# Storing one-hot columns of an adjacency matrix in five transfers, and loading them back on another queue

## The chip, the cores and the metric

The kernel runs on one core of a Trainium2 chip. The metric is the device time of one execution in microseconds (us). TensorE does the matrix products, VectorE and ScalarE move and transform tiles, GpSimd does small powers and indirect gathers, SyncE issues most of the transfers between the core's own memory and DRAM. SyncE and ScalarE each have a queue of their own for transfers; each engine runs its own instructions in program order.

## What is computed

A graph of 3125 nodes and 50000 edges, 256 features per node, four layers with a skip connection:

```python
edge_index = jnp.stack([src, dst])
h = jnp.maximum(_layernorm(x, axis=-1), 0.0)
x = x + _L0_gnn_ref(h, edge_index, ...)   # means over edges, there and back, two times
h = jnp.maximum(_layernorm(x, axis=-1), 0.0)
x = x + _L1_gnn_ref(h, ..., src, dst, edge_type_16)   # sum of messages, then a GRU cell
h = jnp.maximum(_layernorm(x, axis=-1), 0.0)
x = x + _L2_gnn_ref(h, edge_index, ...)   # GCN with self loops, layer norm, relu
h = jnp.maximum(_layernorm(x, axis=-1), 0.0)
x = x + _L3_gnn_ref(h, edge_index, ...)   # attention over four heads
```

## The kernel before

Nodes are cut into 25 tiles of 125. The dense adjacency matrix `k.adj` (125 partitions, 25 row tiles of 3200 bytes, 8-bit floats, 128 bytes for each column tile) stays in the core's memory. It is built from the edge list in `build`; all later stages are in `main`. Every engine has one function there (`sync`, `gpsimd`, `tensor`, `scalar`, `vector`), and what it issues is written out by hand in program order, with semaphores between engines. The stages in `tensor` are, in this order:

- **back1** (13 pairs of tiles, `back1(p)`): products with the transposed adjacency. The transposed tiles are made on the fly. `flip` on TensorE transposes a tile `i` in seven pieces, `flip_out` on ScalarE (even pieces) and VectorE (odd pieces) moves them into slot `i % 4` of `k.big`, and `keep(i)` on SyncE stores the slot to DRAM (`adjTp`) for later use. While `back1(p)` runs, the tiles of pair p+1 are flipped. Before `flip_out` writes the slot again, for tile i+4, it waits for that store (`kept[i % 4]`) and for the products of the pair that read it. On SyncE `store_g(i - 6)` follows each `keep(i)`: two stores of a finished row tile.
- **mean2**, then **back2** (transposed tiles loaded back on ScalarE's queue by `load_at`).
- **gru** with the GRU cell: `cell` on TensorE, then on VectorE `biases(i)`, `cell(i-1)`, `reset(i)`, `low_s(i-1)`, and on ScalarE `gates(i)`, `split_s(i-1)`, `squash(i)`. SyncE stores each finished tile to `x2p` and loads the input of the tile after the next (`load_x1`), and until the tile is number 18, a `load_hold` six tiles ahead.
- **gcn**, with `dense_c`, `turn_h` (a transpose of the normalized tile) and `dense_z` between the products; on VectorE `norm_c(i)`, which needs the tile that `load_x2(i)` brings back from `x2p`. The products that stand before `turn_h` of tile 1 are few, since three pairs begin ahead of time with the tiles that are ready.

Five of the adjacency's column tiles (19 to 23) play a special part. High node numbers get most of the edges, so in mean2 and gru the tiles of high number are summed from gathered rows and one-hot matrices (`far_mean2`, `far_gru`) rather than from the dense columns. The one-hot matrices (`hots`, written by `far_hots` on VectorE) need room, and they take these columns' place, `hot_columns`. So the columns are stored to the DRAM tensor `columns` before mean2 and loaded back before the gcn stage uses them. They are 125 partitions x 25 row tiles x 640 bytes, 2 MB in pieces of 640 bytes. VectorE waits for the semaphore `G["columns"]` before its first `far_hots` and again in the gcn loop at tile 3, where after `one_hots()` it adds the self loops of those columns. The last reader of the one-hot matrices is the last far group of the gru stage (`FAR_TURNS[-1]`, turn 11 of 13); its end is the count `F["used"]` that `copy_out` on ScalarE waits for in that turn.

In the version before, both transfers are issued by SyncE: the store as one transfer (L749) ahead of the loads of `attn_r` and `attn_l` (L751) and `keep(2)`, the load (L793) between `load_x2(0)` and `load_x2(1)` (L734).

Of the kernel before, what the change touches and what calls it, by code (L numbers as in the profile page):

```python
# [26 lines left out]
TILES = NODES // P  # L27
# [134 lines left out]
def visiting():  # L162


    out = []
    for stage, order, tiles in ((0, MEAN_ORDER, range(MEAN_FAR, TILES)), (1, GRU_ORDER, range(FAR, TILES - 1))):
        for turn, tile in enumerate(order):
            if tile in tiles:
                start = out[-1].stop if out else 0
                out.append(Visit(stage, tile, turn, start, start + LISTS[tile - FAR]))  # L170
    return out
# [16 lines left out]
VISITS = visiting()  # L188
# [337 lines left out]
def group_tiles(p):  # L526

    return range(2 * p, min(2 * p + 2, TILES))
# [15 lines left out]
def main(k, built):  # L544


    nc, d = k.nc, k.d
# [14 lines left out]
    def copied_view(n, p):  # L562
        return k.tT[n].rearrange("f c p -> f (c p)").rearrange("f (c x) -> f c x", c=KC)[:, :, 0:P * len(group_tiles(p))]
# [4 lines left out]
    def group_bank(bank, p):  # L568
        return k.ps[0:128, bank, 0:4 * P].rearrange("f (c x) -> f c x", c=KC)[:, :, 0:P * len(group_tiles(p))]
# [9 lines left out]
    whh8 = k.whh[:, :, :].rearrange("f c n -> f (c n)").bitcast(F8)  # L579
    hots = [k.adj_all[:, n % TILES, PITCH * (HOT_AT + n // TILES):PITCH * (HOT_AT + n // TILES) + P] for n in range(GATHERS)]  # L580
    hot_columns = k.adj[:, :, PITCH * HOT_AT:PITCH * (TILES - 1)].bitcast(U32)
    rings = [[whh8[:, 2048 + 1024 * n:2048 + 1024 * (n + 1)].bitcast(F16) for n in range(4)]
             + [k.work[:, 8 * FEAT + FEAT * n:8 * FEAT + FEAT * (n + 1)].bitcast(F16) for n in range(3)]
             + [k.W1[:, n, :].bitcast(F16) for n in range(KC)]
# [20 lines left out]
    def sems(prefix, names):  # L605
        return {n: k.sem(prefix + n) for n in names.split()}
# [6 lines left out]
    F = sems("far_", "hot used")  # L613
# [4 lines left out]
    G = sems("gru_", "columns acc copied turned turned_out product rz read gates pre new x var rstd nmr h hi lo diagonal")  # L618
# [11 lines left out]
    FAR_TURNS = [p for p, g in enumerate(GRU_GROUPS) if FAR <= 2 * g < TILES - 1]  # L630
# [49 lines left out]
    def sync(sp):  # L680

        def keep(i):
            sp.wait_ge(A["flip_a"], evens(NF * (i + 1)))
            sp.wait_ge(A["flip_v"], NF * (i + 1) // 2)
            if i < 4:
                sp.wait_ge(D["root"], 1)
            sp.dma_start(d["adjTp"][i, :, :], k.big[:, ROW * (i % 4):ROW * (i % 4 + 1)].bitcast(U32)).then_inc(kept[i % 4], 16)

        def store_g(i):
            sp.wait_ge(A["lo"], i + 1)  # L690
            for a, b in ((0, 112), (112, P)):
                sp.dma_start(d["pairs"][P * i + a:P * i + b, :], k.pairA[a:b, i, :]).then_inc(M["stored"], 16)

        def store_h(i):
            sp.wait_ge(B["lo"], i + 1)
            for a, b in ((0, 112), (112, P)):
                sp.dma_start(d["pairs"][P * i + a:P * i + b, :], k.pairA[a:b, i, :]).then_inc(M["stored"], 16)

        def load_xh(p):
            if p == 0:  # L700
                sp.wait_ge(A["x"], TILES)
                sp.wait_ge(F["used"], VISITS[VISIT[0, TILES - 1]].stop)
            elif p == 1:
                sp.wait_ge(M["lo"], TILES)
            else:
                sp.wait_ge(B["x"], 2 * p - 2)
            tiles = slice(2 * p, min(2 * p + 2, TILES))
            for buf, src in zip(xbuf[p % 2], (d["x"], d["h0p"])):
                sp.dma_start(buf[:, 0:FEAT * len(group_tiles(p))].rearrange("p (t f) -> p t f", f=FEAT), src[:, tiles, :]
                             ).then_inc(xh_in[p % 2], 16)  # L710
# [19 lines left out]
        def load_x2(i):  # L730
            sp.wait_ge(*((C["x"], i - 1) if i >= 2 else (G["x"], TILES)))
            n = GRU_ORDER.index(i)
            sp.wait_ge(stored[n % 2], turns(n, 1) + 16 * (n // 2 + 1))
            sp.dma_start(k.xin_all[:, FEAT * (i % 2):FEAT * (i % 2 + 1)], d["x2p"][i, :, :]).then_inc(x_in[i % 2], 16)  # L734
# [11 lines left out]
            sp.dma_start(sb, d["b_hh"][FEAT * n:FEAT * (n + 1)].partition_broadcast(P)).then_inc(W["loaded"], 16)  # L746
        sp.wait_ge(built["lo"], TILES)
        sp.wait_ge(built["padded"], 1)
        sp.dma_start(d["columns"][:, :, :], hot_columns).then_inc(G["columns"], 16)  # L749
        for c, name in enumerate(("attn_r", "attn_l")):  # L750
            sp.dma_start(att[:, FEAT * c:FEAT * (c + 1)], d[name].partition_broadcast(128)).then_inc(W["loaded"], 16)  # L751
        for i in range(2, TILES):
            keep(i)
            if i >= 6:
                store_g(i - 6)
            if i == 22:
                sp.wait_ge(W["prepared"], 1)
                sp.dma_start(names.bitcast(I32), d["src_rows"][0:TILES, :]).then_inc(indexed, 16)
# [30 lines left out]
                load_hold(i + len(hold))  # L789

        load_x2(0)
        sp.wait_ge(F["used"], VISITS[-1].stop)
        sp.dma_start(hot_columns, d["columns"][:, :, :]).then_inc(G["columns"], 16)  # L793
        load_x2(1)
        for i in range(TILES):
            if i == 0:
# [387 lines left out]
    def scalar(act):  # L1184
# [19 lines left out]
        def copy_out(S, bank, p, scale=1.0, early=None, far=False):  # L1204
            if far and p in FAR_TURNS:
                act.wait_ge(F["used"], VISITS[VISIT[1, 2 * GRU_GROUPS[p] + 1]].stop)
            else:
                act.wait_ge(S["acc"], p + 1 - far * sum(q < p for q in FAR_TURNS))
            if p >= 2:
                act.wait_ge(S["product"], 2 * p - 2)  # L1210
            elif early is not None:
                act.wait_ge(early, TILES)
            s.activation(copied_view(p % 2, p), group_bank(bank, p), ACT.Copy, scale=scale).then_inc(S["copied"], 1)
# [131 lines left out]
        for p in range(NP):  # L1345
            if p >= 2:
                for i in group_tiles(p - 2):
                    gates(i)
                    if i >= 1:
                        split_s(i - 1)  # L1350
                    squash(i)
            if p >= 1:
                turned_out(p)
            copy_out(G, p % 3, p, CNT / UP, far=True)
        for i in range(2 * NP - 4, TILES):
            gates(i)
            split_s(i - 1)
            squash(i)
# [34 lines left out]
    def vector(dve):  # L1393
# [213 lines left out]
        n = slice(0, TILES)  # L1607
# [39 lines left out]

        dve.wait_ge(A["degree"], 2 * TILES)
        dve.wait_ge(A["flipped"], NF * TILES)
        dve.wait_ge(G["columns"], 16)  # L1650
        for t in range(TILES):
            if t < len(HOT_ORDER):
                far_hots(HOT_ORDER[t])
# [38 lines left out]
        for i in range(TILES):  # L1692
            if i == 3:
                one_hots()
                dve.wait_ge(G["columns"], 32)
                for t in range(HOT_AT, TILES):
                    own_block = k.adj[:, t, PITCH * t:PITCH * t + P]
                    stt(out=own_block, in0=k.ident[:, 0:P], scalar=1.0 / CNT, in1=own_block,
                        op0=ALU.mult, op1=ALU.add, saturate=False).then_inc(G["diagonal"], 1)
            norm_c(i)  # L1700
            if i == 17:
                halves(*PARTS[0])
            if i in (18, 19, 20, 21):
                pick(i - 18, 7)
# [1661 lines left out]
```

## Time and profile before

| | us |
|---|---|
| three runs, median | 1254.53 |
| lowest and highest | 1252.97, 1257.41 |
| profiled execution, span from its first to its last instruction | 1250.3 |
| TensorE busy in it | 1156.4 (92%) |
| VectorE, ScalarE, GpSimd busy | 710.5, 442.8, 362.0 |

The time of a run also holds what lies around the span; the profile shows no total of its own for the profiled execution, and its span is 4.2 us below the median of the runs. Stages by time in the trace: back1 from 291 to 493 us, mean2 to about 605, back2 to about 770, gru to about 1018, gcn to about 1190, the attention to the end. In the page's strip of 40 slices TensorE is at 9 tenths or more nearly throughout, with an 8 at a few places. The traces are read in three steps below: the chain of what ended last tells which engine matters, the timeline of one engine shows what it waited for and how long, and the windows show busy time and granted clock of a stretch.

### The profile page before, as it was taken

Reading aid. Unit: us, or ns where it says so; the run is one execution under the profiler, and the core shown is the slowest. Engines: PE = TensorE matmul, PEld = TensorE weight load, DVE = VectorE, ACT = ScalarE, POOL = GpSimd, SP = SyncE. Lnnn points to the kernel's source line nnn. Section 1 sums busy time; section 2 is a strip of 40 time slices with the busy share of each in tenths; the row PEclk is TensorE's granted clock in tenths of the full one; section 3 lists DMA queues with packets and bytes.
Section 4 is the critical chain, followed back from the end, with each engine's and each line's share of the span. In section 5 each row is a group of like instructions: output and inputs, shape, how many; then the busy total and the mean of one; then the engine's idle time right before and its main releaser. Section 6 shows DMA issues by size and latency. Waiting matters only on the chain.

```text
span 1250.3 us, 23515 instructions
## 1 busy us (share of the span) xinstructions
PE 1156.4 (92%) x9345; PEld 909.1 (73%) x9345; DVE 710.5 (57%) x2020; ACT 442.8 (35%) x948; POOL 362.0 (29%) x546
## 2 busy tenths in 40 slices
PE   1699999998899999999999999999999997999990
PEld 1466666777799988666888888767777675989970
DVE  7876456784566676742255554254546564545566
ACT  3756554437466663212121211221222321122123
POOL 7820000012000000676011112655565211355210
PEclk9999999999899999999999999999999998999995
DMA  4210000003422221433245543333343113122103
GB/s 161 87 35 1 2 1 1 2 1 127 135 71 70 70 71 56 141 102 96 90 166 172 171 158 119 93 102 98 101 123 111 56 35 111 41 59 62 31 10 104
DMA packets 63807, 101.35 MB, mean 81 GB/s; under 512 B 10984, under 2 KB 42339, under 8 KB 63694
## 3 DMA queue, kind: packets, MB, share of 16 engines
q1 hardware_dynamic: 47530, 61.73, 15.2%
q0 software_dynamic: 12032, 27.45, 7.6%
q10 hardware_dynamic: 4132, 10.63, 2.5%
q8 instruction: 75, 1.23, 0.4%
q14 instruction: 38, 0.31, 0.1%
HBM read 64.66 MB, written 35.09 MB: 80 GB/s over the span
## 4 chain that ended last, share of the span: by engine, by line
PE 81%; DVE 6%; DMA 3%; SPq 3%; ACT 2%; POOL 2%; issue 1%; DVEq 0%; ACTq 0%
PE ps L539 33%; PE ps L2157 11%; PE ps L933 8%; PE ps L2181 4%; PE ps L899 3%; PE ps L1031 3%; PE ps L1033 3%; PE ps L888 2%; PE ps L961 2%; DMA xin<-t_x2p 2%; SPq L751 2%; PE ps L1037 2%; PE ps L1035 2%; PE ps L1057 1%; PE ps L946 1%
## 5 line engine op out<-in xcount | busy, mean ns | idle before, releaser
L539 PE MATMUL ps<-big,pairB 125*128 125x250 fp8e4 (+1 forms) x2600 | 304.0, 268 | 0.6 <-DVE big L1405 0.6
L539 PEld LDWEIGHTS ps<-big,pairB 125*128 125x128 f16 x2600 | 239.2, 98 | 30.7 <-issue 3.1
L2157 PE MATMUL ps<-pairA,adj 125*125 125x512 f16 x625 | 207.5, 405 | 0.0
L818 POOL TENSOR_TENSOR st<-st,mhalf 125x1 f32<-125x1 f32 x100 | 61.4, 614 | 345.4 <-DVE st L1525 344.8
L539 PE MATMUL ps<-adj,pairB 125*128 125x250 fp8e4 (+1 forms) x1300 | 147.6, 269 | 1.2 <-DVE pairB L1587 1.2
L539 PEld LDWEIGHTS ps<-adj,pairB 125*128 125x128 f16 x1300 | 123.9, 100 | 16.3 <-DVE pairB L1587 1.5
L2094 ACT ACTIVATE adj<-ps 125x450 fp8e4<-125x450 f32 (+6 forms) x191 | 97.3, 518 | 102.9 <-PE ps L2183 102.5
L2183 PEld LDWEIGHTS ps<-wih 128*128 128x128 bf16 x615 | 84.5, 144 | 51.9 <-issue 1.1
L2183 PE MATMUL ps<-wih 128*128 128x7 bf16 (+5 forms) x615 | 101.9, 178 | 0.0
L933 PE MATMUL ps<-pairA,adj 125*125 125x512 f16 x450 | 98.4, 379 | 0.0
L933 PEld LDWEIGHTS ps<-pairA,adj 125*125 125x125 fp8e4 x450 | 61.6, 137 | 35.2
L539 PE MATMUL ps<-adj,pairA 125*128 125x250 fp8e4 (+1 forms) x800 | 83.7, 265 | 0.0
L539 PEld LDWEIGHTS ps<-adj,pairA 125*128 125x128 f16 x800 | 72.7, 98 | 11.5 <-issue 4.5
L1405 DVE CAST big<-ps 125x500 fp8e4<-125x500 f32 (+1 forms) x87 | 53.7, 625 | 42.1 <-PE ps L888 33.1
L2157 PEld LDWEIGHTS ps<-pairA,adj 125*125 125x125 fp8e4 x625 | 76.1, 139 | 2.1
L842 POOL DMA_INDIRECT whh<-t_pairs,far_src x16 | 15.5, 970 | 213.9 <-DMA t_pairs<-pairA 209.4
L842 POOL DMA_INDIRECT pairB<-t_pairs,far_src x71 | 69.6, 980 | 24.1 <-issue 18.5
L1201 ACT ACTIVATE whh<-adj 125x1625 fp8e4<-125x1625 fp8e4 (+1 forms) x50 | 75.1, 1502 | 0.1
L1871 POOL TENSOR_TENSOR pairB<-work,pairB 125x256 f16<-125x256 f32 x25 | 21.1, 845 | 181.2 <-ACT pairB L2117 181.2
L888 PE MATMUL ps<-identb,adj 125*125 125x125 bf16 x625 | 64.0, 223 | 10.2 <-ACT big L1194 9.3
L1194 ACT ACTIVATE big<-ps 125x500 fp8e4<-125x500 f32 (+1 forms) x88 | 47.2, 542 | 56.0 <-PE ps L888 46.7
L888 PEld LDWEIGHTS ps<-identb,adj 125*125 125x125 fp8e4 x625 | 56.8, 139 | 13.2 <-ACT big L1194 10.0
(334 smaller groups left out, 1953.4 us busy)
## 6 DMA issues: line engine op xcount, KB each, us to landing
t_adjTp<-big SPq DMA_DIRECT2D x25, 400.0 KB, 2.6
big<-t_adjTp ACTq DMA_DIRECT2D x25, 400.0 KB, 3.9
t_pairs<-pairA SPq DMA_DIRECT2D x50, 112.0 KB
t_xh<-work SPq DMA_DIRECT2D x13, 256.0 KB
pairB<-in_x SPq DMA_DIRECT2D x5, 640.0 KB, 9.4
t_h0p<-pairB SPq DMA_DIRECT2D x5, 640.0 KB, 2.9
work<-t_xh SPq DMA_DIRECT2D x25, 128.0 KB, 2.6
xin<-t_xh SPq DMA_DIRECT2D x25, 128.0 KB
```

The source lines that it names most:

```text
L539: last = pe.matmul(out, src[:, j, FEAT * part + 128 * c:FEAT * part + 128 * (c + 1)], rhs(j, p), start=(n + part == 0 and not begun), stop ...
L818: g.tensor_tensor(st[:, 9:10], st[:, 8:9], k.mhalf[:, 0:1], ALU.pow).then_inc(S[rstd], 1)
L842: g.indirect_dma_start(gathered(n), None, d["pairs"], bass.IndirectOffsetOnAxis(ap=k.far_src[:, s:s + 1], axis=0)).then_inc(landed(q)[0], 16)
L888: last = pe.matmul(k.ps[0:P, f % 4, (j - j0) * P:(j - j0 + 1) * P], k.adj[:, i, PITCH * j:PITCH * j + P], k.identb[:, 0:P], start=True, st ...
L933: last = pe.matmul(k.ps[0:P, t % 4, :], k.adj[:, j, PITCH * i:PITCH * i + P], k.pairA[:, j, :], start=(j == 0), stop=(j == TILES - 1))
L1194: s.activation(slots[:, i % 4, j0:j1, 0:P], k.ps[0:P, f % 4, 0:(j1 - j0) * P].rearrange("p (j c) -> p j c", c=P), ACT.Copy, saturate=False ...
L1201: s.activation(junk[:, 0:(j1 - j0) * P].rearrange("p (j c) -> p j c", c=P), cols[:, i, j0:j1, 0:P], ACT.Copy, saturate=False, accum_out=(k ...
L1405: v.tensor_copy(slots[:, i % 4, j0:j1, 0:P], k.ps[0:P, f % 4, 0:(j1 - j0) * P].rearrange("p (j c) -> p j c", c=P), saturate=False).then_in ...
L2094: s.activation(k.adj[:, :, PITCH * i + blk.at:PITCH * i + blk.at + blk.width], k.ps[0:P, BANK[n], 0:blk.width * TILES] .rearrange("p (n j) ...
L2157: last = pe.matmul(k.ps[0:P, 6 + t % 2, :], k.adj[:, j, PITCH * i:PITCH * i + P], k.pairA[:, j, :], start=(j == 0), stop=(j == TILES - 1))
L2181: pe.matmul(k.ps[0:128, BANK[win.block], at:at + TILES * win.width], low, k.hot_keys[m % RING][:, u, 0:TILES * win.width], start=start, st ...
L2183: pe.matmul(k.ps[0:128, 4 + blk.turn % 2, win.at:win.at + win.width], rel, rel[:, RELS:RELS + win.width], start=start, stop=True, skip_gro ...
```

## The change

The store becomes five transfers, each of five row tiles (125 partitions x 5 x 640 bytes), issued after the row stores of tiles 8, 11, 14, 17 and 20 in the back1 stage. The load goes from SyncE's queue to ScalarE's, and stands directly behind `copy_out` of the last far turn. The waits on VectorE count accordingly (80 and 96 in place of 16 and 32). No arithmetic changes.

```diff
+    COLUMN_TURNS = (8, 11, 14, 17, 20)
@@ sync
+        def store_columns(n):
+            part = slice(TILES // len(COLUMN_TURNS) * n, TILES // len(COLUMN_TURNS) * (n + 1))
+            sp.dma_start(d["columns"][:, part, :], hot_columns[:, part, :]).then_inc(G["columns"], 16)
...
         sp.wait_ge(built["padded"], 1)
-        sp.dma_start(d["columns"][:, :, :], hot_columns).then_inc(G["columns"], 16)
         for c, name in enumerate(("attn_r", "attn_l")):
...
             if i >= 6:
                 store_g(i - 6)
+            if i in COLUMN_TURNS:
+                store_columns(COLUMN_TURNS.index(i))
...
         load_x2(0)
-        sp.wait_ge(F["used"], VISITS[-1].stop)
-        sp.dma_start(hot_columns, d["columns"][:, :, :]).then_inc(G["columns"], 16)
         load_x2(1)
@@ scalar
             copy_out(G, p % 3, p, CNT / UP, far=True)
+            if p == FAR_TURNS[-1]:
+                act.dma_start(hot_columns, d["columns"][:, :, :]).then_inc(G["columns"], 16)
@@ vector
-        dve.wait_ge(G["columns"], 16)
+        dve.wait_ge(G["columns"], 16 * len(COLUMN_TURNS))
...
-                dve.wait_ge(G["columns"], 32)
+                dve.wait_ge(G["columns"], 16 * len(COLUMN_TURNS) + 16)
```

SyncE, head of the back1 stage, before. `t_columns<-adj` is the store of the columns, `t_adjTp<-big` are the stores of the flipped tiles, `t_pairs<-pairA` those of the finished rows:

```order
L746 DMA gates_b<-in_b_hh 125x256
L749 DMA t_columns<-adj 3125x1x160
L751 DMA work<-in_attn_r 128x256
L751 DMA work<-in_attn_l 128x256
L687 DMA t_adjTp<-big 128x800 x5
L692 DMA t_pairs<-pairA 112x512
L692 DMA t_pairs<-pairA 13x512
```

SyncE, the same place and on to the first of the five transfers, of the changed kernel:

```order
L752 DMA gates_b<-in_b_hh 125x256
L756 DMA work<-in_attn_r 128x256
L756 DMA work<-in_attn_l 128x256
L688 DMA t_adjTp<-big 128x800 x5
L693 DMA t_pairs<-pairA 112x512
L693 DMA t_pairs<-pairA 13x512
L688 DMA t_adjTp<-big 128x800
L693 DMA t_pairs<-pairA 112x512
L693 DMA t_pairs<-pairA 13x512
L688 DMA t_adjTp<-big 128x800
L693 DMA t_pairs<-pairA 112x512
L693 DMA t_pairs<-pairA 13x512
L703 DMA t_columns<-adj 125x5x160
```

The long store has gone from ahead of `attn_r` and the first five tile stores; a fifth of it stands behind the row stores that follow tile 8, and four more come three tiles apart.

SyncE, from the end of the gru stage to the gcn stage, before (`xin<-t_x2p` are the loads `load_x2`, `CT<-t_lists` the broadcast that `one_hots` needs):

```order
L785 DMA t_x2p<-work 128x256
L734 DMA xin<-t_x2p 128x256
L793 DMA adj<-t_columns 125x25x160
L734 DMA xin<-t_x2p 128x256
L799 DMA CT<-t_lists 128x3125
```

ScalarE, gru stage, turn 11, of the changed kernel (L1218 is `copy_out`, L1270 the first `gates` after it):

```order
L1265 COPY W2<-ps 128x500
L1218 ACTIVATE work<-ps 128x500
L1361 DMA adj<-t_columns 125x25x160
L1270 ACTIVATE big<-big 125x512
L1283 ACTIVATE ho<-ho,st1 125x256
```

On SyncE the load of tile 1's input now follows that of tile 0's directly, and the columns' load stands on ScalarE between `copy_out` of turn 11 and `gates(20)`.

## Rows read from the trace of the kernel before

**Rows 1.** The page, part 4: chain that ended last, by engine.

```profile
PE 81%; DVE 6%; DMA 3%; SPq 3%; ACT 2%; POOL 2%; issue 1%; DVEq 0%; ACTq 0%
```

**Rows 2.** Timeline of SyncE's queue, 302 to 339 us: start, duration, line, transfer, count.

```profile
302.39 2.82 SPq L749 DMA_DIRECT2D t_columns<-adj  x1
305.26 21.17 SPq L751 DMA_DIRECT2D work<-in_attn_r  x1
...
327.03 11.74 SPq L687 DMA_DIRECT2D t_adjTp<-big  x5
```

**Rows 3.** Timeline, 332 to 333 us; in brackets idle before, and what ended it.

```profile
332.09 1.07 ACT L1194 ACTIVATE big<-ps 125x500 fp8e4<-125x500 f32 x2 [9.28 <-DMA t_adjTp<-big]
...
332.74 0.69 PE L888 MATMUL ps<-identb,adj 125*125 125x125 bf16 x4 [6.02 <-ACT big L1194]
```

**Rows 4.** VectorE's timeline: the last piece of an odd tile, once per pair.

```profile
306.24 0.29 DVE L1405 CAST big<-ps 125x125 fp8e4<-125x125 f32 x1 [1.11 <-PE ps L888]
...
321.80 0.29 DVE L1405 CAST big<-ps 125x125 fp8e4<-125x125 f32 x1 [1.11 <-PE ps L888]
...
345.82 0.29 DVE L1405 CAST big<-ps 125x125 fp8e4<-125x125 f32 x1 [1.11 <-PE ps L888]
```

**Rows 5.** Windows: length, busy by engine, granted clock (PEclk), DMA share, GB/s.

```profile
333.00:337.00 4.00, 4.00 (x20) 3.08 (x20) 1.79 (x5) 3.60 (x6) 0.00 (x0) 0.50 0.19 70
345.80:361.40 15.60, 15.60 (x161) 14.12 (x160) 10.53 (x23) 10.70 (x18) 0.00 (x0) 1.00 0.21 72
1056.40:1061.10 4.70, 4.23 (x20) 3.07 (x21) 4.35 (x14) 1.14 (x3) 1.93 (x3) 0.50 0.09 28
```

**Rows 6.** SyncE's queue in steady back1: end of one tile's stores, next tile's.

```profile
362.08 0.97 SPq L692 DMA_DIRECT2D t_pairs<-pairA  x2
369.98 0.34 SPq L687 DMA_DIRECT2D t_adjTp<-big  x1
```

**Rows 7.** SyncE's queue at the head of the gcn stage.

```profile
1030.82 0.84 SPq L793 DMA_DIRECT2D adj<-t_columns  x1
...
1031.77 15.79 SPq L734 DMA_DIRECT2D xin<-t_x2p  x1
...
1047.67 0.37 SPq L799 DMA_DIRECT2D CT<-t_lists  x1
```

**Rows 8.** Timeline of three engines in the gcn stage, 1051 to 1065 us.

```profile
1051.09 1.13 PE L1057 MATMUL ps<-Wg,work 128*125 128x256 f32 x4 [0.68 <-ACT work L1213]
1053.48 0.43 DVE L1601 SCALAR_TENSOR_TENSOR pairA<-big,xin 125x256 f32<-125x256 f32 x1 [5.38 <-DMA xin<-t_x2p]
...
1054.75 0.47 DVE L1592 SCALAR_TENSOR_TENSOR big<-ps,dinvs,bg 125x256 f32<-125x256 f32 x1
...
1056.41 0.68 PE L1066 MATMUL ps<-ident,ho 125*128 125x125 f32 x2 [4.20 <-ACT ho L1287]
...
1060.50 0.60 ACT L1287 ACTIVATE work<-pairA,st 125x256 f32<-125x256 f32 x1 [1.74 <-POOL st L824]
...
1064.65 0.38 PE L1066 MATMUL ps<-ident,work 125*128 125x125 f32 x2
```

**Rows 9.** Timeline of the gru stage, from turn 11 to the first gcn products.

```profile
992.25 0.63 ACT L1265 ACTIVATE big<-big 125x512 f32<-125x512 f32 x1
...
995.18 0.38 SPq L728 DMA_DIRECT2D xin<-t_xh  x1
...
995.58 0.42 DVE L1566 TENSOR_TENSOR big<-big 125x256 f32<-125x256 f32 x1
...
1007.88 0.69 DVE L1554 TENSOR_TENSOR big<-ps,gates_b 125x512 f32<-125x512 f32 x1 [2.50 <-PE ps L1037]
...
1009.15 0.42 DVE L1573 TENSOR_TENSOR big<-work,big 125x256 f32<-125x256 f32 x1
...
1033.53 6.19 PE L539 MATMUL ps<-adj,pairB 125*128 125x250 fp8e4 x56 [1.18 <-DVE pairB L1587]
```

**Rows 10.** The page, part 6: a load of a tile, its size and its landing.

```profile
work<-t_xh SPq DMA_DIRECT2D x25, 128.0 KB, 2.6
```

## The prediction

> **What bounds the kernel now.** The chain of what ended last comes first: four fifths of it is TensorE [rows 1]. So a transfer is worth something only where TensorE stands still for it, and the rest of the reading is a search for such places around the two transfers that the change moves. There are two.
>
> The first is in back1. SyncE's queue issues the columns' store at 302.4; the issue itself takes 2.8 us, but the next transfer in the queue, the small `attn_r`, then holds SyncE for 21.2 us, until 326.4 [rows 2]. Behind it stand the stores of the flipped tiles 2 to 6, which start at 327.0. The tile that takes slot 2 again (tile 6) cannot be moved out of PSUM before the store of tile 2 has landed: ScalarE waits 9.3 us for it, up to 332.1, and TensorE 6.0 us, up to 332.7 [rows 3]. After that TensorE runs at half clock for some 5 us (0.50 from 333 to 337, against 1.00 in an undisturbed pair) [rows 5].
>
> The second is at the head of the gcn stage. The columns' load takes 0.84 us to issue, and the next transfer, tile 1's input, holds the queue for 15.8 us, to 1047.6 [rows 7]. VectorE waits 5.4 us for that input, up to 1053.5, and TensorE 4.2 us for the normalized tile, up to 1056.4 [rows 8]; then it is again at the lower level, 1.2 GHz in place of 2.4, with 4.23 us of work done by 1061.1 [rows 5].
>
> **Part one, the store.** What it is worth is read best from the pace. The last piece of an odd tile passes VectorE once per pair: at 306.24, 321.80 and 345.82 [rows 4]. One undisturbed pair takes 15.56 us, the disturbed one 24.02. The difference, 8.5 us, holds the standstill and the slow clock together, and nothing else differs between the pairs. TensorE is busy all the time in an undisturbed pair [rows 5], so I let the full 8.5 us go.
>
> What is late next? With the store gone, `attn_r`, `attn_l` and tile 2's store are issued at about 303, as soon as the tile is there, nearly 20 us before slot 2 is wanted at 322. Nothing takes the stall's place.
>
> The five short stores are the added cost. The long one held its queue 2.8 + 21.2 = 24 us for 3125 pieces of 640 bytes, 7.7 ns a piece; a fifth of that is 4.8 us for each. In steady back1 the row stores of a tile end at 363.05 and the next tile's store is issued at 369.98 [rows 6], a gap of 6.9 us, or about 5.9 in the shorter of the two alternating steps (an estimate: two steps make a pair of 15.6 us and differ by about 1 us). So each short store fits in between. And if it did not: a slot is written again one and a half pairs after its store is due, some 23 us, so each of the five could be late by more than 15 us before TensorE noticed. I take zero; the bounds are zero and, if each made one tile store late enough to cost as much as it holds the queue, 5 x 4.8 = 24 us, which the slack rules out unless it is wrong by a factor of four. VectorE's wait for all five comes at the end of back1 near 493 us; the fifth goes out near 440 in the new count. Zero as well.
>
> **Part two, the load leaves SyncE's queue.** Tile 1's input can then be issued at 1030.8 and lands in about 2.6 us [rows 10], long before VectorE wants it at 1048.1 (1053.48 less its wait of 5.38). The normalized tile is then ready at about 1051.7: 5.3 us sooner than 1056.4, which would be 1051.1, but ScalarE first has to finish its `copy_out`, which ends 0.05 us before the product at 1051.09 [rows 8], and then needs 0.6 us. TensorE is busy with that product until 1052.2. So the 4.2 us go completely. With them goes the slow clock: 4.23 us of work at 0.50 [rows 5] take 2.1 us at full clock. Gain 6.3 us.
>
> What is late next is the tile after. Its VectorE part begins when the product ends, 1052.2; before it took from 1054.75 to the end of ScalarE's step at 1061.10, 6.35 us, which gives 1058.6. TensorE would come to its transpose after 1064.65 - 1056.41 - 2.1 = 6.1 us, at 1058.3 [rows 8]. That is a new wait of 0.3 us. VectorE then has the 3.2 us of `one_hots` and self loops before tile 3, much closer to the time when tile 3 is wanted than before; I count nothing for it, with 1.5 us as the bound. Part two gives 6.3 - 0.3 = **6.0 us**. The broadcast that `one_hots` needs follows the freed queue to about 1032, so it has landed long before.
>
> **Part three, the load on ScalarE's queue.** The issue stands behind the `copy_out` of turn 11 and before `gates(20)`, which began at 992.25. Taken from the same transfer on SyncE it costs 0.84 us of ScalarE [rows 7]; the store's 2.8 us [rows 2] is the upper bound. `gates(20)` takes 0.63 and its reader on VectorE starts at 995.58 [rows 9]: 2.7 us of room. At 0.84 nothing is lost; at 2.8 us some 0.1 us, and VectorE has 2.5 us of idle time ahead of 1007.88 to take it up. Queued behind this issue on ScalarE is only `gates(20)` and what follows; no further transfer is issued there until the end, so there is none that it could hold. The data: 17 us from 992.4 puts the landing near 1010, and the self loops want it at about 1059. Zero. The far groups' gathers have landed by then, as `copy_out` waits for their last use, and the last `load_hold` goes out at tile 18, before 992.
>
> What runs beside it on SyncE's queue are the stores to `x2p` and the loads of inputs; the first load is issued at 995.18 and its tile is read at 1009.15 [rows 9], 14 us later, with 2.6 us needed.
>
> **Sum.** 8.5 + 6.0 = 14.5 us. The profiled span of 1250.3 becomes 1235.8. It lies 4.2 us below the median of the runs, and that stays: **1240.0 us**.
>
> **The rivals.**
>
> *The two queues share what makes the pieces.* SyncE was held by the piece-making of its own transfer, and no row shows what the other queue does meanwhile. If SyncE's transfers stand still from 992.4 until the load's pieces are made, 0.84 + 15.79 us later, that is 1009.0. Then come the pending store (0.32), the input of tile 21 (0.38) and 2.6 us to land: 1012.3 against a need at 1009.15. From there VectorE has no idle time to the end of the stage, and TensorE waits for its last tile [rows 9], so 3.2 us are lost, and up to 2.1 more if TensorE's pause, 1.18 + 3.2 us, brings the low clock again, as the pauses of 6.0 and 4.2 did. Time: 1243.2 to 1245.3. For it: the hold of 15.8 us happened on a transfer of an ordinary kind. Against it no row speaks. The Trainium skill, "DMA: Bandwidth & Descriptors", section "Queues, rings and completion order", says that SP and ACT each own a row of rings on the same 16 engines, "not a DMA engine or descriptor generator of their own"; taken literally this is the rival. The same page's section "Issuing engines are not separate DMA queues" says that issuing from two engines only saves time on the sequencer; the trace agrees that it was the issuing sequencer's time, 15.79 us of it, that hurt here. Chance 0.22.
>
> *VectorE becomes the late one in the gcn stage.* The tile after tile 1, then `one_hots`, then tile 3 follow with hardly any room. If each is late by half a microsecond or more, 1 to 2.5 us of part two come back: 1241.0 to 1242.5. Chance 0.12.
>
> *ScalarE is held through the load.* If not the next transfer but the issuing engine itself stands still until about 1009, the reader at 995.58 moves to 1009.9, 14.3 us later; VectorE's idle 2.5 us takes part of it up, so 11.8 remain, and about 2.1 for the clock: 1253.9, no change. Against it: the issue on SyncE ended after 0.84 us and the next instruction was reached. Chance 0.03.
>
> *A longer run at full clock is not granted.* The change takes away two pauses of TensorE. If the chip answers unbroken work with the lower level, in the stretch from 291 to 493 where the pause at 327 is gone, the cost is half of the time spent there: from 29 us at half clock on, the whole gain is lost, and 40 us give 1260. Against it: the pair after the pause has full clock with TensorE busy for all of its 15.6 us [rows 5], and back1 goes on like that for nine pairs. Chance 0.02.
>
> *The change does only half.* If the tile stores were still late for another reason (the weight loads ahead of them in the queue), part one would fail and 1248.5 be left. Against it: those loads had been issued by 302 and the queue moved on. Chance 0.02.
>
> **How the numbers follow.** The forecast has 0.59 with its own range of 1238 to 1242: half a microsecond of reading error in each part, and 1.5 us of scatter, as the runs before spread from 1253.0 to 1257.4. The range must take in the shared queue and the late VectorE: 1237.5 to 1245.5 leaves out less than 0.15. About 0.3%, 4 us, is what a measurement of this kernel can tell from no change. Faster by more than that, below 1250.8: 0.59 + 0.22 + 0.12 + 0.02 = 0.95, less 0.01 for what I have not thought of: 0.94. Within it 0.04, slower 0.02.
>
> **What would show it.** After the change, the odd tile's last piece should pass VectorE every 15.6 us from 306 on, with no wait for a tile store and a granted clock of 1.00 through 345. The transfer behind each short store should be held for under 5 us. Tile 1's input should be issued within 1 us of tile 0's, TensorE should not wait over 1 us before the transpose of tile 1, and the clock should stay at 1.00 there. In the gru stage the input load after turn 11 should be issued in 0.4 us; if it takes over 10, the queues share, and VectorE will wait for tile 21's input. If TensorE pauses in the gcn stage at tile 2 or 3 for over 1 us, VectorE has become late. A clock below 1.00 in a stretch without a pause would make the whole sum wrong.

## The result and the profile after

| | before | after |
|---|---|---|
| median of four runs, us | 1255.2 | 1240.92 |
| lowest and highest, us | 1252.97, 1257.41 | 1239.74, 1241.23 |
| profiled span, us | 1250.3 | 1236.6 |
| TensorE busy in the span, us | 1156.4 | 1152.3 |

The ratio is 0.989 with a 95% interval of 0.9874 to 0.9906: the changed kernel is faster by 1.1%. The forecast was 1240.0 us. It started from a before of 1254.53, the median of three runs; the before above has a fourth run of 1255.87 and a median 0.7 higher. The page of the changed kernel, parts 1 and 4 (busy time of each engine; the chain that ended last, by engine):

```profile
PE 1152.3 (93%) x9345; PEld 906.8 (73%) x9345; DVE 710.6 (57%) x2020; ACT 442.9 (36%) x948; POOL 361.9 (29%) x546
...
PE 85%; DVE 7%; ACT 3%; POOL 2%; issue 1%; DMA 1%; DVEq 0%; ACTq 0%
```

In [rows 1] the chain had 3% of SyncE's queue and 3% of DMA. The first is gone and the second down to 1%. TensorE's share of the chain has gone up by 4 points because the span is shorter and the two stops are out of it. The gain in time has two parts: about 9.6 us in which TensorE stood still, and 4 us that it worked less, since the same matmuls ran at a higher clock.

**Place one, the head of back1.** VectorE's timeline of the changed kernel, the last piece of an odd tile:

```profile
306.60 0.29 DVE L1412 CAST big<-ps 125x125 fp8e4<-125x125 f32 x1 [1.11 <-PE ps L893]
...
322.16 0.29 DVE L1412 CAST big<-ps 125x125 fp8e4<-125x125 f32 x1 [1.11 <-PE ps L893]
...
337.67 0.29 DVE L1412 CAST big<-ps 125x125 fp8e4<-125x125 f32 x1 [1.11 <-PE ps L893]
```

The pair that took 24.02 us in [rows 4] takes 15.51. SyncE's queue, timeline from 302 us on (start, duration, line, transfer, count):

```profile
302.19 2.87 SPq L756 DMA_DIRECT2D work<-in_attn_r  x1
305.10 0.43 SPq L756 DMA_DIRECT2D work<-in_attn_l  x1
305.65 25.48 SPq L688 DMA_DIRECT2D t_adjTp<-big  x5
...
347.72 0.30 SPq L703 DMA_DIRECT2D t_columns<-adj  x1
353.55 0.34 SPq L688 DMA_DIRECT2D t_adjTp<-big  x1
...
442.63 0.30 SPq L703 DMA_DIRECT2D t_columns<-adj  x1
447.62 0.34 SPq L688 DMA_DIRECT2D t_adjTp<-big  x1
```

The long row of five tile stores is no hold: it begins at 305.65 and includes the waits for tiles 3 to 6; taken singly, none of the five takes over 0.36 us. The stores behind the short transfers are issued in 0.34 us when their tile is ready. Even in the tightest case, the fifth, 4.69 us lie between the end of the issue and the next store, and nothing of a hold is left by then.

**Place two, the head of the gcn stage.** SyncE's queue and TensorE there in the changed kernel:

```profile
1022.15 0.96 SPq L740 DMA_DIRECT2D xin<-t_x2p  x2
```

```profile
1042.95 1.13 PE L1062 MATMUL ps<-Wg,work 128*125 128x256 f32 x4 [0.68 <-ACT work L1218]
1043.91 0.38 PE L1071 MATMUL ps<-ident,ho 125*128 125x125 f32 x2
...
1050.52 0.43 PE L1071 MATMUL ps<-ident,work 125*128 125x125 f32 x2 [0.20 <-ACT work L1292]
```

Tile 0's and tile 1's inputs are issued in one row of 0.96 us, where [rows 7] had 15.79 for the second alone. The transpose of tile 1 follows without a wait, and that of tile 2 waits 0.20 us. Windows of the changed kernel over both places (length, busy PE, PEld, DVE, ACT, POOL, granted clock, DMA share, GB/s):

```profile
333.00:337.00 4.00, 4.00 (x42) 3.60 (x40) 2.98 (x6) 2.21 (x4) 0.00 (x0) 1.00 0.05 18
...
1043.90:1050.50 6.60, 5.96 (x49) 4.88 (x47) 5.89 (x19) 1.14 (x3) 2.09 (x3) 1.00 0.07 20
```

[rows 5] had 0.50 at both: 20 matmuls in the 4 us from 333 to 337, and here 42 in a stretch of the same length.

**Place three, the load on ScalarE's queue.** Timeline of the gru stage in the changed kernel:

```profile
982.70 0.89 ACTq L1361 DMA_DIRECT2D adj<-t_columns  x1
...
982.85 0.40 ACT L1274 ACTIVATE big<-big 125x256 f32<-125x256 f32 x1
...
984.09 0.63 ACT L1270 ACTIVATE big<-big 125x512 f32<-125x512 f32 x1
...
986.60 0.32 SPq L792 DMA_DIRECT2D t_x2p<-ho  x1
...
987.01 0.38 SPq L734 DMA_DIRECT2D xin<-t_xh  x1
```

The issue takes 0.89 us of ScalarE's queue, and ScalarE computes during it (the ACTIVATE at 982.85 runs from then to 983.25, inside 982.70 to 983.59). `gates(20)` stands at 984.09, which is 8.16 us before its place in [rows 9]; the first gcn product is earlier by 8.15, and back1 began 0.36 later in this execution (306.60 against 306.24), so neither lost anything of the 8.51 us from place one. SyncE's transfers go out in 0.32 and 0.38 us while the load is under way on the other queue.

### The profile page after: what moved, and what is told of

Same layout as the page of the kernel before. It is cut to its first block, busy times and chain, and to the rows that moved or that the text cites. A ratio compares the mean times of both kernels' runs of the same rounds, so it can differ in the third digit from the quotient of the medians.

```text
span 1236.6 us, 23519 instructions
## 1 busy us (share of the span) xinstructions
PE 1152.3 (93%) x9345; PEld 906.8 (73%) x9345; DVE 710.6 (57%) x2020; ACT 442.9 (36%) x948; POOL 361.9 (29%) x546
## 4 chain that ended last, share of the span: by engine, by line
PE 85%; DVE 7%; ACT 3%; POOL 2%; issue 1%; DMA 1%; DVEq 0%; ACTq 0%
PE ps L539 35%; PE ps L2164 12%; PE ps L938 8%; PE ps L2188 4%; PE ps L904 3%; PE ps L1036 3%; PE ps L1038 3%; PE ps L893 3%; PE ps L966 2%; PE ps L1062 2%; PE ps L1042 2%; PE ps L1040 2%; PE ps L951 1%; PE ps L994 1%; POOL st L823 1%
```

## The experiments

The theory: a long transfer does not hold its own issue, but the transfer instruction that stands next behind it on the same engine; it costs time only if that next one is wanted within the hold. The main rivals were that the two queues share the hold, that cutting the store is what helps, and that the second queue is what helps. The diffs are against the kernel before, unless their first line names another kernel, and show the moved transfers alone; where `store_columns` appears, it is the function of the change, and the counts of the waits follow.

### One half at a time

```diff
# e1_short_stores: five stores at tiles 8, 11, 14, 17, 20; load left on SyncE
-        sp.dma_start(d["columns"][:, :, :], hot_columns).then_inc(G["columns"], 16)
+            if i in COLUMN_TURNS:
+                store_columns(COLUMN_TURNS.index(i))
# e2_act_load: store left as it was; load on ScalarE's queue
-        sp.dma_start(hot_columns, d["columns"][:, :, :]).then_inc(G["columns"], 16)
+            if p == FAR_TURNS[-1]:
+                act.dma_start(hot_columns, d["columns"][:, :, :]).then_inc(G["columns"], 16)
```

> Only the five short stores; the load back stays on SyncE's queue between the loads of tiles 0 and 1. Theory: the two parts are independent, the first is worth 8.5 us (one pair of back1 took 24.02 us in place of 15.56), so 1246.7 against 1255.2 before, with TensorE's 4.2 us wait in the gcn stage unchanged. Rival: the two gains overlap, or a part of the second stall is due to the first, and the time is over 1 us from that.

Measured: 1246.96 us (1245.71 to 1250.15), ratio 0.9931 (0.9906 to 0.9955).

> Only the load back on ScalarE's queue; the long store stays at the head of back1. Theory: worth 6.0 us, so 1249.2 against 1255.2, with the 6.0 us wait at the start of back1 unchanged. Rival: less than 5 us, because of a cost of the transfer on ScalarE that the first part covers.

Measured: 1247.08 us (1246.85 to 1250.18), ratio 0.9925 (0.9906 to 0.9943), 2.1 us below what was expected. With the five stores alone, SyncE's queue and TensorE at the head of the gcn stage read:

```profile
1022.37 0.93 SPq L800 DMA_DIRECT2D adj<-t_columns  x1
1023.40 15.72 SPq L740 DMA_DIRECT2D xin<-t_x2p  x1
```

```profile
1047.84 0.68 PE L1073 MATMUL ps<-ident,ho 125*128 125x125 f32 x2 [3.96 <-ACT ho L1294]
```

With the moved load alone, TensorE's timeline has the stop of back1 and not that of gcn:

```profile
333.94 0.69 PE L886 MATMUL ps<-identb,adj 125*125 125x125 bf16 x4 [5.95 <-ACT big L1192]
...
1059.54 0.43 PE L1064 MATMUL ps<-ident,work 125*128 125x125 f32 x2 [0.20 <-ACT work L1285]
```

Each edit takes away its own stop and leaves the other as it was, so the two terms of the sum are separate. For the moved load the traces give 5.98 us: from the cast in back1 (307.52 here, 306.24 before) to tile 2's transpose it is 752.02 us instead of 758.41, and 0.41 of that belongs to the pair in back1, 23.61 for 24.02. The execution traced is the slowest of the four, 1250.18 us. By the runs the two edits gave 9.2 and 9.1 us against a before of 1256.18, with some 3 and some 2 us to either side. That would be 18.3 together, where both at once give 14.3. The before of this comparison is 1 us higher than the one above, which counts twice here; the rest is of the size of the intervals. So the runs show that each edit gives something, and the traces how much.

### Is it the cut into five, or the place?

```diff
# e5_five_at_head: all five short stores where the long one was; load on ScalarE
-        sp.dma_start(d["columns"][:, :, :], hot_columns).then_inc(G["columns"], 16)
+        for n in range(len(COLUMN_TURNS)):
+            store_columns(n)
# e4_one_at_turn8: the whole store behind tile 8; load on ScalarE
-        sp.dma_start(d["columns"][:, :, :], hot_columns).then_inc(G["columns"], 16)
+            if i == 8:
+                sp.dma_start(d["columns"][:, :, :], hot_columns).then_inc(G["columns"], 16)
```

> As the changed kernel, but the five short stores stand one after another at the head of back1, where the long one was. Theory (the queue is held by the total of pieces behind which a transfer stands): the hold of about 24 us is back, only spread, and with it 8.5 us: 1249.4 against 1240.9 of the changed kernel. Rival (the hold belongs to the size of one transfer, so splitting alone cures it): 1240.9.

Measured: 1247.67 us (1246.47 to 1249.83), ratio 0.9932 (0.9909 to 0.9954).

> As the changed kernel, but the store is one transfer of 2 MB, issued on SyncE's queue behind tile 8's row stores, where the first short one is. Theory (a slot is written again some 23 us after its store is due; the hold is 24 us, less the 6 us of gap): tile 9's store is late by about 17 us, within the slack, and nothing is lost: 1240.9. So the place is what counts, and the split is not needed. Rival: the slack is smaller than I read, TensorE stops as at 327 us, and up to 8 us come back.

Measured: 1240.61 us (1238.05 to 1241.3), ratio 0.9888 (0.9868 to 0.9908). SyncE's queue with the five stores at the head (all five in one row, then the second, third and fifth singly, and the transfer behind), and TensorE's stop:

```profile
301.48 20.30 SPq L703 DMA_DIRECT2D t_columns<-adj  x5
304.42 5.98 SPq L703 DMA_DIRECT2D t_columns<-adj  x1
310.44 3.80 SPq L703 DMA_DIRECT2D t_columns<-adj  x1
318.17 3.61 SPq L703 DMA_DIRECT2D t_columns<-adj  x1
321.82 3.82 SPq L758 DMA_DIRECT2D work<-in_attn_r  x1
```

```profile
332.11 0.68 PE L893 MATMUL ps<-identb,adj 125*125 125x125 bf16 x4 [4.14 <-ACT big L1199]
```

The five hold the queue for 20.30 + 3.82 = 24.1 us together, the same as the one long store with 24.0 [rows 2], only spread over more rows. So cutting the store by row tiles does not shorten the hold of its data. But the hold of one fifth is not 24.1 / 5 = 4.8 us: from the second fifth on, what stands behind a fifth takes 3.80, 3.84 (the fourth), 3.61 and 3.82 us. The rest of the 24.1 lies in the first fifth, whose own row takes 2.90, and the second, 5.98, at the place where the queue comes from other loads. SyncE reached this place 0.9 us sooner and back1 began 1.3 us later than in the trace of before, which is why the stop is shorter, 5.7 us with the clock (21.22 us for the pair less 15.51). The whole store behind tile 8:

```profile
348.63 0.95 SPq L762 DMA_DIRECT2D t_columns<-adj  x1
354.48 12.00 SPq L688 DMA_DIRECT2D t_adjTp<-big  x1
```

It holds the next tile's store for 12 us, to 366.5, and TensorE and ScalarE have no wait for a tile store there. The place alone gives the whole of part one. From the start of its issue to the release of the queue it is 17.9 us here, where the same store took 24.0 at the head of back1. The 6.1 us between them belong to that place and not to the store; the changed kernel's `attn_r`, which is the first there, also takes 2.87 us to issue with no store ahead of it. Whether the loads ahead of it (L742 to L746) are the cause was not tested.

### How late may a tile store be?

```diff
# e10_store_twice: e4_one_at_turn8 with a second store to a DRAM tensor of its own
             if i == 8:
                 sp.dma_start(d["columns"][:, :, :], hot_columns).then_inc(G["columns"], 16)
+                sp.dma_start(d["columns2"][:, :, :], hot_columns).then_inc(G["columns"], 16)
```

> The changed kernel, but the 2 MB store goes out whole at tile 8, and then a second time to another DRAM tensor: an added transfer, to find how long tile 9's store can be late before TensorE stands still. With one store tile 9's was held until 366.5 us and nothing stopped. Two transfers hold for 0.9 + 17 us each by that trace, so tile 9's store is issued at about 384 and lands at about 387. Theory (the slack of some 23 us that the prediction counted, from 354.5 to about 377): ScalarE waits some 9 us for the store of tile 9, TensorE some 6 us, then half clock for some 5 us, 8 to 9 us lost in all: 1249 to 1250 us. If each holds 24 us, as at the head of back1, the loss is 20 us or more: 1261 us. Rival (the slack is larger than two pairs, 31 us): no wait, 1241 us.

Measured: 1252.93 us (1251.51 to 1254.08, ten runs), ratio 0.9985 (0.9973 to 0.9997). SyncE's queue, ScalarE and TensorE, from their timelines:

```profile
347.99 16.89 SPq L763 DMA_DIRECT2D t_columns<-adj  x1
364.99 20.14 SPq L688 DMA_DIRECT2D t_adjTp<-big  x1
```

```profile
390.30 1.07 ACT L1200 ACTIVATE big<-ps 125x500 fp8e4<-125x500 f32 x2 [12.37 <-DMA t_adjTp<-big]
...
391.15 0.69 PE L894 MATMUL ps<-identb,adj 125*125 125x125 bf16 x4 [9.71 <-DVE big L1413]
```

It is 12.3 us above e4_one_at_turn8. Tile 9's store leaves at 385.1, 1 us later than expected. ScalarE wanted it landed at 390.30 - 12.37 = 377.9. In the changed kernel that store goes out at 353.55 in an execution that began 0.7 us later, so it was due at 352.8 here, 25.1 us before it was wanted landed. A tile store takes 2.6 us to land (`t_adjTp<-big`, 400.0 KB, in part 6 of the changed kernel's page), so it may be late by 22.5 us. The prediction had "some 23" for the time from due to wanted, and had not taken the landing off. The time came out 3 us above the 1249 to 1250 of the theory, for a reason the rows show: the store took 5.2 us to land instead of 2.6, and the clock stayed low for longer. Windows of this kernel:

```profile
388.00:392.00 4.00, 0.84 (x6) 0.79 (x7) 1.58 (x4) 1.70 (x3) 0.00 (x0) 0.50 0.98 347
392.00:396.00 4.00, 4.00 (x24) 3.11 (x22) 2.81 (x8) 1.69 (x4) 0.00 (x0) 0.50 0.08 28
396.00:400.00 4.00, 4.00 (x39) 3.61 (x38) 2.02 (x6) 1.76 (x4) 0.00 (x0) 0.83 0.40 134
```

Four held tile stores and their row stores go out at once from 385 to 391 and fill all the engines (share 0.98).

### Do the two queues share the hold?

```diff
# e6_store_on_act: the whole store on ScalarE's queue in back1, turn 1; load on ScalarE too
-        sp.dma_start(d["columns"][:, :, :], hot_columns).then_inc(G["columns"], 16)
+            if p == 1:
+                act.wait_ge(built["padded"], 1)
+                act.dma_start(d["columns"][:, :, :], hot_columns).then_inc(G["columns"], 16)
```

> As the changed kernel, but the store is one transfer of 2 MB again, issued on ScalarE's queue at the second pair of back1, about 307 us. Theory (a transfer holds only what stands behind it on its own queue): no stall, 1240.9, tile stores on SyncE's queue issued in their usual 0.3 us during it. Rival (both queues share what makes the pieces): the tile stores wait some 20 us, 1249.4.

Measured: 1240.07 us (1238.89 to 1242.14), ratio 0.9872 (0.985 to 0.9894). Both queues in its timeline:

```profile
305.38 0.91 ACTq L1314 DMA_DIRECT2D t_columns<-adj  x1
305.64 25.17 SPq L688 DMA_DIRECT2D t_adjTp<-big  x5
```

The five tile stores take 25.17 us with the waits for their tiles, as in the changed kernel (25.48), although the same 2 MB leave from the same moment on the other queue; singly, none takes over 0.36 us in either. The hold is not shared, but the way out is: from issue to landing the tile stores between 300 and 345 us took 3.1 to 9.3 us, 6.0 in the middle, where the changed kernel has 2.3 to 8.2 and 2.8. TensorE and ScalarE have no wait for them there. Next, the same load left on SyncE, where it meets the gru stage's transfers:

```diff
# e3_load_sp_gru: as the changed kernel, but the load on SyncE behind turn 11's last use
+            if i == 19:
+                sp.wait_ge(F["used"], VISITS[-1].stop)
+                sp.dma_start(hot_columns, d["columns"][:, :, :]).then_inc(G["columns"], 16)
```

> As the changed kernel, but the load is issued in the gru stage on SyncE's queue, ahead of the store of the 20th finished tile (994.8 us by the clock of the kernel before). This makes on purpose what the rival of the shared queues would have done. Theory: SyncE is held for about 16 us, the input of tile 21 arrives at about 1014 by that clock (994.8 + 16.6 + 0.3 + 2.6) where 1009.2 is the need, so 3 to 5 us are lost, and up to 2 more if TensorE's clock drops in the pause: 1244 to 1248. Rival: VectorE has more room than I see, and it stays at 1240.9.

Measured: 1247.59 us (1246.99 to 1248.79), ratio 0.9946 (0.9929 to 0.9962), 6.7 us above the changed kernel. Its SyncE queue, VectorE and TensorE:

```profile
986.08 0.92 SPq L794 DMA_DIRECT2D adj<-t_columns  x1
987.05 15.92 SPq L795 DMA_DIRECT2D t_x2p<-ho  x1
1003.09 0.36 SPq L734 DMA_DIRECT2D xin<-t_xh  x1
```

```profile
1007.47 0.43 DVE L1581 TENSOR_TENSOR big<-work,big 125x256 f32<-125x256 f32 x1 [6.93 <-DMA xin<-t_xh]
```

```profile
1013.16 15.82 PE L539 MATMUL ps<-adj,pairB 125*128 125x250 fp8e4 x132 [3.68 <-DVE pairB L1595]
...
1031.87 7.84 PE L539 MATMUL ps<-adj,pairB 125*128 125x250 fp8e4 x56 [2.90 <-DVE pairB L1595]
```

This is what the rival of the shared queue would have looked like. In these runs the hold is there when the next transfer stands on the same engine (15.92 us), and absent when it stands on the other (0.32 us in the changed kernel). So ScalarE's queue was a good place for the load at that time, and SyncE's a bad one.

### Is a second queue needed?

```diff
# e9_load_sp_later: five short stores; load on SyncE, behind the lists' broadcast
# e8_order_alone: one whole store behind tile 8; load as in e9_load_sp_later
         load_x2(0)
-        sp.wait_ge(F["used"], VISITS[-1].stop)
-        sp.dma_start(hot_columns, d["columns"][:, :, :]).then_inc(G["columns"], 16)
         load_x2(1)
...
                 sp.dma_start(one_hot, d["lists"].rearrange("t p -> (t p)").partition_broadcast(128)).then_inc(T["lists"], 16)
+                sp.wait_ge(F["used"], VISITS[-1].stop)
+                sp.dma_start(hot_columns, d["columns"][:, :, :]).then_inc(G["columns"], 16)
```

> As the changed kernel, but the load is on SyncE's queue again, only later than before: behind the loads of tiles 0 and 1 and behind the broadcast of the lists. Theory: the hold of about 16 us now falls on tile 2's input. It is issued at about 1040.4 by the changed kernel's clock and lands by 1043.5, before VectorE wants it at 1046.8; the columns land by 1042, before the self loops at 1050.0. So no loss, 1240.9: the order on one queue was enough. Rival: the broadcast of 0.8 MB and the columns delay each other, or tile 2's input is late, and 1 to 5 us are lost.

Measured: 1239.46 us (1238.76 to 1239.87), ratio 0.9881 (0.9864 to 0.9897).

> The kernel before, with its two 2 MB transfers whole and both on SyncE's queue, only moved: the store behind the row stores of tile 8, the load behind the lists' broadcast at the head of the gcn stage. Nothing is cut and no second queue is used. Theory (what matters is only which transfer stands next behind a long one, and when that one is wanted): 1240.9 us, the time of the changed kernel, with the odd tiles' casts every 15.6 us and TensorE waiting under 1 us before the transpose of tile 1. Rival (the cut into five, or the second queue, is worth something of its own that the single edits did not show): 1243 us or more. Were the two gains not to add up, 1247 us.

Measured: 1240.89 us (1239.86 to 1241.5), ratio 0.9887 (0.9861 to 0.9913). SyncE's queue of the latter:

```profile
1023.41 0.93 SPq L740 DMA_DIRECT2D xin<-t_x2p  x2
1024.44 0.38 SPq L804 DMA_DIRECT2D CT<-t_lists  x1
1024.87 0.83 SPq L806 DMA_DIRECT2D adj<-t_columns  x1
```

Two transfers in another place, whole and on one queue, give all that the change gives. Behind the load the next transfer, tile 2's input, was not to be issued before 1037.8 (in the changed kernel, without the load, its row begins at 1036.53), so the hold falls on it alone: taken singly its issue takes 4.98 us, to 1042.8. TensorE's wait at tile 2's transpose stays 0.20 us (0.40 in e9_load_sp_later). All versions between 1239.5 and 1240.9 have intervals that overlap: none is shown to beat the changed kernel.

### What makes the hold so long?

```diff
# e7_split_112: the kernel before, nothing moved, both transfers cut by partitions
-        sp.dma_start(d["columns"][:, :, :], hot_columns).then_inc(G["columns"], 16)
+        for a, b in ((0, 112), (112, P)):
+            sp.dma_start(d["columns"][a:b, :, :], hot_columns[a:b, :, :]).then_inc(G["columns"], 16)
```

> The kernel before, with both transfers at their old places on SyncE's queue, each cut by partitions into 112 and 13. The Trainium skill (DMA: Bandwidth & Descriptors, section on why a DMA increments its semaphore by 16) says that a transfer's engines number the largest divisor up to 16 of its slowest dimension: 5 for 125, 16 for 112. The DMA share of 0.35 during both transfers before fits 5 of 16. Theory (engines set the hold): the holds of 24 and 16.6 us fall to about a third, the tile stores are issued by about 311 and tile 1's input by about 1037, both in time: 14.5 us gained with nothing moved, 1240.9. Rival (the number of pieces alone sets the hold, 7.7 ns each): no change, 1255.2.

Measured: 1240.14 us (1240.08 to 1241.77), ratio 0.9888 (0.9871 to 0.9904). Its SyncE queue at both places:

```profile
301.55 11.01 SPq L750 DMA_DIRECT2D t_columns<-adj  x2
312.60 1.31 SPq L752 DMA_DIRECT2D work<-in_attn_r  x1
...
1023.61 5.26 SPq L795 DMA_DIRECT2D adj<-t_columns  x2
1028.98 0.91 SPq L734 DMA_DIRECT2D xin<-t_x2p  x1
```

And a window of this kernel, then one of the kernel before, both inside the store:

```profile
305.00:309.00 4.00, 3.96 (x44) 3.48 (x43) 2.05 (x5) 2.89 (x6) 0.00 (x0) 1.00 1.06 333
```

```profile
307.00:311.00 4.00, 4.00 (x47) 3.76 (x45) 2.01 (x6) 2.35 (x4) 0.00 (x0) 1.00 0.34 116
```

The same bytes pass at 333 GB/s in place of 116, and the hold falls from 24.0 to 12.3 us for the store (11.01 + 1.31) and from 16.6 to 6.2 for the load (5.26 + 0.91). For the store 6.1 us of both figures are again those of its place, so its own part falls from 17.9 to about 6.2, by the same factor of 2.9 as the rate. With them the tile stores began at 315.1 and not at the expected 311, still in time: TensorE waits for none. The busy share was 0.34 of 16 engines, 5.4 of them, before, and is 1.06 here (a share can come out a little above 1: all of them). The Trainium skill, "DMA: Bandwidth & Descriptors", section "Why a DMA increments its semaphore by 16 and not by 1", says under "How many engines (k)" that a transfer uses the largest number up to 16 that divides the outer sizes of both its sides. By that rule it is 5 for 125 rows, 16 for 112 and 13 for 13; the trace agrees, by its 0.34 before and by the factor of 2.9 in the rate (5 engines would be 0.31, and 16 for 5 a factor of 3.2).

So there is a third way to the same gain: the prediction's 7.7 ns a piece is not the price of making a piece. Away from the head of back1 it is 17.9 us for 3125 pieces, 5.7 ns, and the same pieces go through in about a third of that once the cut lets more engines work on them.

## Why the prediction was right

**Part one, 8.5 us forecast, 8.51 in the traces** (24.02 less 15.51). Its reasoning, that the pace of a pair holds standstill and slow clock together, holds as it stands. "Nothing takes the stall's place" held too: TensorE has no wait for a tile store in the rest of the stage.

**The short stores, zero forecast, nothing seen.** The hold of each was sized too high: 4.8 us is a fifth of 24, and 6.1 of the 24 belong to the head of back1. The fifths in e5_five_at_head hold 3.6 to 3.8 us, and the whole store behind tile 8 holds 17.9. The forecast did not depend on it. The gap was sized too high as well: from the end of the row stores to the next tile store, 5.9 us were taken for the shorter step, and the tightest of the five is 5.0 (442.59 to 447.62). So a fifth fits everywhere, by a wider margin than 4.8 us would have. Behind that stands the slack: 25.1 us from due to wanted, of which a store may be late by 22.5.

**Part two, 6.0 us forecast, 5.98 in the traces.** Tile 2's transpose went from 1064.65 to 1050.52, 14.13 us; 8.15 of these were there before the stage began, and 5.98 are its own. The new wait was put at 0.3 and is 0.20.

**Part three, zero forecast, zero seen.** The price of the issue was right, 0.89 for 0.84; the step that it takes time from ScalarE was not needed, since ScalarE computed during it.

**The rest of the sum.** At tile 2 of the gcn stage the changed kernel is 14.13 + 0.36 = 14.49 us ahead, counted from the same cast in back1; the forecast had 14.5. The spans differ by 13.7, or 14.1 counted so, thus 0.4 us are given back between there and the end, at no place that I can name. The medians differ by 14.3. The time itself came out 0.9 us above the forecast, and 0.7 of that is the before, which moved up with its fourth run.

**The rivals.** *The shared queue* (0.22) is refuted, as far as the hold goes, by e6_store_on_act and by the rows at 986.60 and 987.01. What it describes was made to happen in e3_load_sp_gru, by putting the load on SyncE. It cost 6.7 us by the runs and 7.0 by the trace (first gcn products 725.79 us after the cast in back1, against 718.78), at the upper end of what was expected, though not for the reason given. VectorE reads tile 21's input at 1007.47 there, 7.0 us late counted from the cast. Of that, 3.9 are the place: on SyncE the load goes out 680.0 us after the cast, on ScalarE 676.1. The remaining 3.1 is, by this count, what the same hold would have cost the changed kernel, and the prediction had 3.2. It was a sum of two errors that cancel: the landing took 4.0 us instead of 2.6, and the load goes out 1.5 us earlier than I had set it. The 2.1 us for the low clock added nothing visible; the clock did fall (0.68 granted over the 5 us from 1013), but VectorE was the late one, and TensorE waited for it again at 1031.87.

*VectorE late in gcn* (0.12): no; from 1050 to 1090 TensorE works 39.80 of 40 us at a clock of 1.00. *ScalarE held*: no. *No longer run at full clock*: no; the granted clock is 1.00 over the whole stretch from 291 to 493 and in the gcn stage to 1180. *Only half*: no.

**What was only assumed.** That the hold is a matter of making pieces was not shown by any row, and e7_split_112 puts another cause in its place. The sum did not depend on it, since it was made from the length of the hold alone; the chance of 0.22 for the shared queue did.

## What to carry to other kernels

Where a queue shows a long hold, look one transfer ahead of the one that bears it: here the cause was the long transfer before it, and moving that behind transfers that were wanted soon cost nothing and gave all of the gain. Do not take the whole length of a hold for the price of its transfer: of the 24.0 us here, 6.1 came with the place. Before cutting or moving it, look at the DMA share beside GB/s: 0.34 of 16 engines at 116 GB/s was the sign that the row count, 125, kept most engines out, and a cut into 112 and 13 rows gave the same 14 us with nothing moved. Price a pause of TensorE by the pace of the loop it stands in (24.02 against 15.56 us), which takes in the slow clock behind it, and price a late transfer by when it is issued and how crowded the engines are when it lands (2.6 us here in calm, 4.0 to 5.2 behind a backlog).

## What I had not expected of the hardware

- A transfer issued on ScalarE cost ScalarE nothing: its 0.89 us ran while an ACTIVATE of 0.40 us at 982.85 computed, and 0.91 us in back1 (e6_store_on_act) ran beside one of 0.59 us at 305.37. No later step of TensorE came late by it.
- Cutting off 13 of 125 partitions let the same bytes through 2.9 times as fast.
- A backlog has a price of its own: the held stores leave together, and the one that is waited for took twice its usual time to land (5.2 us for 2.6).
- The two queues do not hold each other's issue, but a 2 MB store on the one doubled the landing of tile stores on the other (6.0 us in the middle for 2.8).
